# Relation passes of a graph network with more gather buffers, one-hots and pairs of PSUM banks

## The reference, cut to what matters

```
h = jnp.einsum('ni,rio->rno', x, W)
msg = h[etype, src]
seg = dst * num_rels + etype
sums = jax.ops.segment_sum(msg, seg, num_segments=N * num_rels)
cnt = jax.ops.segment_sum(jnp.ones(msg.shape[0], x.dtype), seg, num_segments=N * num_rels)
mean = sums / jnp.maximum(cnt, 1.0)[:, None]
agg = mean.reshape(N, num_rels, do).sum(axis=1)
return agg + x @ W_root + b
```

## Time and profile before

| what | us |
|---|---|
| median of 3 runs | 3812.71 |
| lowest and highest run | 3811.78, 3816.45 |
| the profiled execution, its own time | 3823.57 |
| its span, first to last instruction | 3821.7 |
| PE busy in the span | 2532.7 |
| DVE busy in the span | 2517.1 |
| POOL busy in the span | 1959.8 |
| ACT busy in the span | 485.3 |

### The profile page before, as it was taken

One profiled execution on the slowest core, in us unless ns is written; L12 is line 12 of the kernel. 1 busy time (PEld: TensorE's weight loads), 2 busy tenths in 40 slices (PEclk: granted clock), 3 DMA queues, 4 the chain that ended last, 5 costly groups with the idle time before them and its releaser, 6 DMA issues.

```text
span 3821.7 us, 59833 instructions
## 1 busy us (share of the span) xinstructions
PE 2532.7 (66%) x21427; PEld 1819.2 (48%) x21427; DVE 2517.1 (66%) x6311; ACT 485.3 (13%) x906; POOL 1959.8 (51%) x2108
## 2 busy tenths in 40 slices
PE   3766689989746565666555558965555655656556
PEld 1222265574435444444444446754444444444446
DVE  5999954464267666666666666666666666666667
ACT  2444441151110000000000003510000000000000
POOL 1887800000256666666666662146666666666661
PEclk9999989989865666566666668966666666666667
DMA  1000000000111111111111111111111111111111
GB/s 51 1 1 1 1 6 1 1 2 1 39 52 44 45 44 45 44 45 44 45 45 45 45 45 49 75 60 44 45 44 45 44 45 44 45 45 45 44 45 32
DMA packets 76098, 137.92 MB, mean 36 GB/s; under 512 B 29902, under 2 KB 44640, under 8 KB 75810
## 3 DMA queue, kind: packets, MB, share of 16 engines
q0 software_dynamic: 53120, 108.90, 10.9%
q1 hardware_dynamic: 18934, 24.46, 1.8%
q10 hardware_dynamic: 3756, 0.73, 0.2%
HBM read 116.35 MB, written 17.62 MB: 35 GB/s over the span
## 4 chain that ended last, share of the span: by engine, by line
PE 45%; DVE 28%; issue 11%; another core or an unknown queue 8%; POOL 3%; DMA 2%; ACT 2%; DVEq 1%; ACTq 1%; SPq 0%; POOLq 0%
PE banks L565 26%; DVE adj L1429 15%; DVE hi_hot L1131 6%; PE banks L497 6%; PE banks L490 3%; DVE lo_hot L1139 3%; PE banks L609 2%; POOL adj L711 2%; PE banks L621 2%; DMA adj<-table,adj 2%; PE banks L654 1%; DVEq L1427 1%; PE banks L472 1%; POOL lo_hot L685 1%
## 5 line engine op out<-in xcount | busy, mean ns | idle before, releaser
L565 PE MATMUL banks<-adj 128*128 128x129 f16 x13280 | 1486.3, 291 | 1026.5 <-DVE adj L1429 739.7
L711 POOL DMA_INDIRECT adj<-table,adj x1660 | 1573.3, 948 | 946.8 <-issue 402.1
L565 PEld LDWEIGHTS banks<-adj 128*128 128x128 f16 x13280 | 1199.5, 132 | 1317.9 <-issue 1161.6
L1429 DVE TENSOR_TENSOR adj<-adj,banks 128x516 f32 x1660 | 1143.0, 689 | 844.5 <-PE banks L565 480.7
L1413 DVE TENSOR_SCALAR adj<-adj 128x512 f16<-128x512 f16 x1660 | 697.1, 420 | 0.0
L685 POOL TENSOR_SCALAR lo_hot<-minus_iota,zT 128x128 f16<-128x128 f16 x392 | 332.4, 865 | 140.4 <-PE banks L445 77.1
L445 PE MATMUL banks<-hi_hot,lo_hot 128*128 128x400 f16 x977 | 267.0, 365 | 128.0 <-DVE hi_hot L1131 73.5
L1131 DVE TENSOR_SCALAR hi_hot<-iota,zT 128x400 f16<-128x400 f16 x977 | 266.0, 338 | 21.5 <-PE banks L445 21.4
L692 POOL MEMSET adj<- 128x1548 f16 x1 | 1.4, 1388 | 470.4 <-PE banks L497 470.4
L445 PEld LDWEIGHTS banks<-hi_hot,lo_hot 128*128 128x128 f16 x977 | 97.4, 100 | 297.9 <-issue 240.4
L497 PE MATMUL banks<-adj,split 128*128 128x512 f16 (+1 forms) x1190 | 235.7, 356 | 0.0
(11 more groups left out here) (219 smaller groups left out, 1625.6 us busy)
## 6 DMA issues: line engine op xcount, KB each, us to landing
adj<-table,adj POOLq DMA_INDIRECT x1660
table<-adj SPq DMA_DIRECT2D x25, 512.0 KB, 2.6
table<-split SPq DMA_DIRECT2D x6, 256.0 KB, 2.3
out_dram<-xres SPq DMA_DIRECT2D x6, 256.0 KB
adj<-in_L_gnn_W_dram SPq DMA_DIRECT2D x1, 1024.0 KB, 7.4
adj<-in_L_gnn_W_dram SPq DMA_DIRECT2D x2, 512.0 KB, 9.0
adj<-scr_index SPq DMA_DIRECT2D x1, 830.0 KB
scr_index<-adj SPq DMA_DIRECT2D x1, 512.0 KB
```

The costliest lines, as they stand in the source:

```text
L565: m = e.matmul(ps[:, g * CH // 2:g * CH // 2 + b - a], hot[:, s, g * P:g * P + P], gath[:, s, a:b], start=(q == 0), stop=(q == 1), skip_gr ...
L711: e.indirect_dma_start(gath[:, s, 0:2 * D], None, table, bass.IndirectOffsetOnAxis(ap=index[:, which, j:j + 1].bitcast(U32), axis=0)).then ...
L1429: e.tensor_tensor(a, a, ps[:, :].rearrange("p (g d) -> p g d", g=G)[:, :, 0:D + 1], ALU.add).then_inc(accumulated, 1)
```

## The change

- `NG`, the gather buffers, are 12 and no longer 6.
- `hot` has its own count of slots, `NH` = 8, and `AHEAD` is 6 and no longer 4.
- Pairs of PSUM banks: four in pass 1. In pass 0 three up to step 127, and four from step 128 (`PAIR_FROM`) on, when the square sums have left banks 6 and 7; there the matmuls wait once for `bound_set` and, for four steps, for the accumulate of step 127. The function `pair_of` gives the pair and the step whose accumulate empties it.
- Memory: `place` moves to another stretch of SBUF (that of the dense stage's tensors), `parts` stands ahead of `ones_all`.
- On POOL the memset of `place` and its four copies move from ahead of pass 0 to behind the clearing of the sums, ahead of pass 1.

```
-AHEAD = 4
+AHEAD = 6
...
-        NG = 6
-        NPAIR = 3
+        NG, NH = 12, 8
+        PAIR_FROM = 128
...
-        hot = carve([P, NG, G * P // 2], F16)
+        hot = carve([P, NH, G * P // 2], F16)
...
-        place = carve([P, REL, P])
...
+        place = sb("place", [P, REL, P], F32, rel)
...
+        def pair_of(which, j):
+
+            if which == 0 and j < PAIR_FROM:
+                return j % 3, j - 3
+            j0 = 0 if which else PAIR_FROM
+            return (j - j0) % 4, j - 4 if which or j >= PAIR_FROM + 4 else PAIR_FROM - 1
...
-                    if j >= NPAIR:
-                        e.wait_ge(accumulated, base + j - NPAIR + 1)
-                    ps = pair[j % NPAIR]
+                    k, emptied = pair_of(which, j)
+                    if which == 0 and j == PAIR_FROM:
+                        e.wait_ge(bound_set, 6)
+                    if emptied >= 0:
+                        e.wait_ge(accumulated, base + emptied + 1)
+                    ps = pair[k]
...
-                            m = e.matmul(ps[:, g * CH // 2:g * CH // 2 + b - a], hot[:, s, g * P:g * P + P],
+                            m = e.matmul(ps[:, g * CH // 2:g * CH // 2 + b - a], hot[:, j % NH, g * P:g * P + P],
...
-                s, base = j % NG, which * JR
-                if base + j >= NG:
-                    e.wait_ge(scattered, base + j - NG + 1 if j >= NG else base)
+                s, base = j % NH, which * JR
+                if base + j >= NH:
+                    e.wait_ge(scattered, base + j - NH + 1 if j >= NH else base)
...
-                    ps = pair[j % NPAIR]
+                    ps = pair[pair_of(which, j)[0]]
```

More of the change, by code:

```diff
@@ L225, in gnn_stack @@
         w2_r = w2.rearrange("p (h r d) -> p h r d", r=RR, d=D)
+        parts = carve([P, 2, REL * 2, D // 2], F16)
         ones_all = carve([P, P])
-        parts = carve([P, 2, REL * 2, D // 2], F16)
         w1p = sb("w1p", [P, 2, RR, H], F16, rel)
@@ L694, in _ @@
                    allow_small_or_imprecise_dtypes=True).then_inc(rel_set, 1)
[L695 to L701, removed]
             e.memset(ones_all[:, :], 1.0).then_inc(ones_set, 1)
@@ L722, in _ @@
                 e.memset(sums_g[:, nb * GB:(nb + 1) * GB, :], 0.0).then_inc(sums_zero, 1)
+            e.memset(place[:, :, :], 0.0).then_inc(own_pool, 1)
+            e.wait_ge(own_pool, 1)
+            for a in range(0, P, WR):
+                for w in range(WPB):
+                    e.tensor_copy(place[a:a + WR, w * G:(w + 1) * G, w * WR:(w + 1) * WR],
+                                  ident[a:a + WR, a:a + WR].unsqueeze(1).broadcast_to([WR, G, WR])).then_inc(place_set, 1)
+                    e.wait_ge(place_set, a // WR * WPB + w + 1)
             for s in range(2):
```

## The result

The changed kernel takes 3881.74 us (median of 4 runs, 3875.30 to 3884.79), the kernel before beside it 3814.24: a ratio of 1.0175, 95% interval 1.0157 to 1.0193. It is 67 us slower. The forecast was 3800, and the time lies above the upper end of the range, 3840.

The account below looks back on a forecast made before the run. Late PE marks, held back by long streams of gathers, were taken to bound the kernel. Buffers -6, pairs -8 and switch +1 summed to -13 us, from a median of 3812.71 to 3800; range 3680 to 3840.

Parts of the forecast that it names:

- What bounds the kernel: Both relation passes: no engine is full; long streams of gathers delay PE's marks, making the pace 1.50 us a step.
- No DMA is added or moved; the tensors only lie at other addresses: Memory layout of the whole kernel: the moved addresses were given no cost in the sum.
- `NG` at -6: Twelve gather buffers, both passes: cover half the cost of POOL's own pauses, -6 us, ends 0 and -12.
- Longer streams [...] hardly change the pace: Gathers in both passes: runs longer than five, which more buffers allow, keep nearly the same time a step.
- Four pairs at -8: PSUM pairs, 1532 steps: cycles of six or seven steps at 1.487 instead of 1.492 us a step, -8 us.
- One-hots 0: DVE's eight one-hots, six ahead: the extra ones before each pass lie under the table wait, zero; uncovered 1.7 us.
- the switch +1: Step 128 of pass 0: PE's matmuls wait for accumulate 127, between 0 and +2 us, taken as +1.
- `place` 0: POOL's memset and copies moved ahead of pass 1: hidden under the table wait, zero; uncovered +2.7 us.
- (a): Rival, both passes: the three pairs are the limit, so four reach POOL's 1.25 us a step, 3431 us; chance 0.15.
- (b): Rival: POOL's wait stays that of a run of five, 1.452 us a step, 3746; with paces up to (a), chance 0.15.
- (c): Rival: long streams hold marks longer than they save, 1.507 us a step in every cycle, +23, 3836 us; chance 0.15.
- the likeliest case: The main forecast for the whole kernel: 3775 to 3818 us, given a chance of 0.55.

Follow-up runs that it names:

- late sets: Sets of runs in which the unchanged kernel before took 3785 to 3820 us; in the other kind it took 3412 to 3416.
- free stream: Kernel before, gathers sent to an unread ring, PE multiplying constant rows without waiting for them: 5152.78 us against 3785.69; in another set 3215.61 against 3414.00.

## Why the prediction was wrong

**What bounds the kernel: right for late sets.** "A long stream of gathers holds back the completion of matmuls" is shown: with gathers one mark in 22 to 28 us, with memsets none held, after the gathers none held. Two things were missing. It holds in some sets of runs only. And "it comes when the stream of gathers stops" was too strong: while the seventeen gathers of after run without a stop, two marks come, 5.0 us apart.

**The step that failed: "No DMA is added or moved; the tensors only lie at other addresses", a term put at nothing without a reason.** With `win` at its new address DVE's load of 32 registers takes 7.13 us instead of 2.10, 52 times. DVE stands still for that time, and with it PE's pairs, the marks and POOL. The cycle of 32 steps shows 43 of the 57 us by which the two profiles differ, and the excess stands at the very gather that waits for the load. The prediction has no row on the loads. That it is the load is shown by where the pauses stand: they move with the number of buffers and pairs as the program has it, in four kernels, and with four buffers they are 110 of 114 us. No run moves `win` alone.

**`NG` at -6, and "Longer streams [...] hardly change the pace".** The buffers cost 143 us alone and 67 with the rest, not -6. The sentence itself is not refuted in the steady part: outside the loads the gathers come 1.466 us apart in after and 1.448 with twelve buffers alone, where the forecast for all was 1.487. But one term of the lead was not in my sum. The lead of twelve must be worked off behind the last gather of each pass: +7.5 and +6.1 us, which the rows of before could have told, as DVE's own pace of 0.94 times six more steps is 5.6. That is 14 of the 57. The runs of fours and sixes are another account of the same 47 us and not a cause. At the average of before's fives (1.464 a step) the fours and sixes cost 63 x (6.26 - 4 x 1.464) + 79 x (9.08 - 6 x 1.464) = 49 us, where it was 8 for before's, while their medians haven't grown.

**Four pairs at -8: nothing by itself.** With six buffers the change is -4 us, inside the interval. "At each release up to four steps are ready, so a cycle has six steps or seven" came true in part: with six buffers and four pairs there are 101 runs of six beside 182 of five, where before, in another set, has 36 and 254, and still no gain. In after five are most frequent. Beside twelve buffers four pairs help: 1.0175 with them, 1.0382 without, in different sets. The gather that waits for the load comes 3.37 us behind its predecessor with four pairs and 5.08 with three.

**One-hots 0, the switch +1, `place` 0: right as a sum,** as the same experiment holds them all.

**The rivals.** (a) and (b) did not occur. (c), slower because long streams hold the marks longer than they save, had the right sign, a chance of 0.15 and a third of the size: +23 where +67 was measured. The sign was luck, for its reason is not the one that the traces show. Its condition was that the step from the last start of a run of six to the next is over 2.70 us. In after it is 9.08 - 6.25 = 2.83 on average over 79 runs, but 2.68 in the median run, so the average meets it by some long runs. The row of before, 2.74, had met it too; I had written that this was close. The range ended just above (c), with no term for the lead and none for the addresses. And 3818, the upper end of the likeliest case, doesn't follow from the bounds given: 1.497 a step makes it 3815, or 3821 with nothing for `NG`.

**What stays open.** Why a load takes 2.10 or 7.13 us, beyond that it goes with the place of `win`. What twelve buffers would do in a late set with a load of 2.10 us. And what makes a set late: chip, machine and time of day can't be told apart by the record, and every execution on record comes with the profiler's span and clock, so that a part of the profiler itself in it is not ruled out. The Trainium skill, "Perfetto Trace Analysis", section "Tensor Engine Instruction (MATMUL, LD_WEIGHTS)", has PE push its semaphore update when PSUM has acknowledged. In the other kind of sets the trace agrees, with 0.014 us from the modelled end to the mark; the free stream in a late set has up to 82.5 us from the end of the matmuls to DVE's start, and PE's own rows show none of it.

## What to carry to other kernels

A buffer that grows moves every tensor behind it. Compare the duration of every instruction before and after, those of the sequencers too, which a page of busy times leaves out: here the code of the load was the same, and its time was 3.4 times as long. A pause that comes every n steps points at work that is done every n steps; fold the starts by n, and work out from the program which step has to wait for it. A deeper ring covers such a pause where its lead lasts longer than the pause does. It costs its lead once behind the last item of each pass. And a gap between the pitch of the busiest engine (here 1.25 us) and the pace (1.50) that no wait for work explains may go with the set of runs; then the change has to be judged in both kinds.

## What the runs showed of the hardware

- A load of 32 registers from SBUF by DVE's sequencer took 2.10 us with the row at one place and 7.13 us at another, in every run. In the two layouts with the fast load the row starts at a multiple of 16 bytes in its tensor, in the three with the slow one it doesn't; that this is the rule is not tested.
- The same kernel takes 3412 to 3416 us in some sets and 3785 to 3820 in others, 11 to 12% apart. The kernel after has accumulates of 689 ns and gathers of 0.94 us in both, and matmuls of 277 ns in the late set and 267 in the other.
- In late sets an unbroken stream of gathers (128 rows of 512 bytes each) settles at 1.40 us a gather and lets one mark of PE through in 16 or 20 gathers; the program with the free stream takes 5153 us there and 3216 in another set. The gathers' packets take the same time in both (0.24 us for 4096 bytes). It is the updates of semaphores that are late: held marks stand 0.092 us apart in the record, where no two are under 0.45 in the other sets.
- A one-hot on DVE takes 751 ns beside memsets on POOL and 350 without. The Trainium skill, "SBUF — State Buffer", section "SBUF: two separate sides", says that DVE, in some of its modes, and GpSimd share a port pair that is locked for a whole instruction. The trace is in line with a lock; in which mode the one-hot ran it doesn't tell. The accumulates (673 ns, where they have 689 beside gathers) show none of it.
